# One more step of the first sort on TensorE, 17 fewer scattered columns on GpSimd, and the feed-forward weights loaded earlier, in parts

## The reference

```python
edge_index = jnp.stack([src, dst])
x = x + _L0_gnn_ref(_layernorm(x, axis=-1), edge_index, L0_gnn_W, L0_gnn_a_l, L0_gnn_a_r)   # attention on the graph
x = x + _L0_ffn_ref(_layernorm(x, axis=-1)[None], ...)[0]      # feed-forward on the selected nodes
x = x + _L1_gnn_ref(_layernorm(x, axis=-1), src, dst, edge_type_4, self_W, self_b, rel_W)   # 4 relations
x = x + _L1_ffn_ref(_layernorm(x, axis=-1)[None], ...)[0]      # 8 experts, 2 per node
# attention on the graph, with h = (x @ W) split in 4 heads, row = src and col = dst:
e = jax.nn.leaky_relu(hl[row] + hr[col], negative_slope=ALPHA)
ee = jnp.exp(e - e_max[row])
att = ee / segment_sum(ee, row)[row]
out_h = segment_sum(att[:, :, None] * h[col], row)
# feed-forward: the 1561 of 3125 rows with the greatest weight x @ wr + br
h = gelu(sel @ w1 + b1);  y = (h @ w2 + b2) * w_sel
```

## Time and profile before

| | before |
|---|---|
| median of three runs | 1993.55 us (1991.79 to 1993.94) |
| the profiled execution, own time | 1998.76 us |
| its span | 1997.0 us |
| busy PE / DVE / ACT / POOL | 1437.6 / 1302.2 / 569.5 / 1391.3 us |
| mean granted clock of TensorE | 0.85 of full speed |
| attention's gathers (464) | 447.4 us busy, 964 ns of one |
| scattered columns of sort a (119) | 150.5 us busy, 1265 ns of one |
| chain that ended last | POOL 38%, PE 19%, DVE 17%, issue 15%, DMA 9% |

### The profile page before, as it was taken

The page is one execution under the profiler, slowest core; times in us unless marked ns, Lnnn a source line. Parts: engine busy times, 40 slices in busy tenths (PEclk is TensorE's granted clock), DMA queues, the critical chain, the costliest instruction groups (busy, mean ns, idle before and its releaser), DMA issues.

```text
span 1997.0 us, 22558 instructions
## 1 busy us (share of the span) xinstructions
PE 1437.6 (72%) x6235; PEld 944.4 (47%) x6235; DVE 1302.2 (65%) x2919; ACT 569.5 (29%) x1670; POOL 1391.3 (70%) x1400
## 2 busy tenths in 40 slices
PE   5666267788888887569999967766666776457980
PEld 3333045665565555447775434333333333256870
DVE  6999477788898887475995035445444444666544
ACT  0687211146566663032332311000000000242220
POOL 0788777777777777778875457777777777546771
PEclk9799678889999999779999979889877777557995
DMA  5111034444444444802003573333333333412337
GB/s 92 12 31 28 6 102 108 108 105 118 119 119 118 119 104 119 107 17 62 1 2 83 142 220 105 105 106 105 105 106 106 105 106 104 46 52 72 102 103 213
DMA packets 105960, 183.76 MB, mean 92 GB/s; under 512 B 31722, under 2 KB 70077, under 8 KB 105714
## 3 DMA queue, kind: packets, MB, share of 16 engines
q0 software_dynamic: 56928, 134.61, 27.9%
q1 hardware_dynamic: 47603, 45.16, 8.6%
q10 hardware_dynamic: 1308, 2.56, 0.5%
HBM read 151.56 MB, written 30.39 MB: 91 GB/s over the span
## 4 chain that ended last, share of the span: by engine, by line
POOL 38%; PE 19%; DVE 17%; issue 15%; DMA 9%; DVEq 1%; ACT 1%; SPq 0%; POOLq 0%; ACTq 0%
POOL gath L891 29%; POOL slot_tab L711 8%; PE ps L925 6%; DMA gath<-y_tab,index_b 4%; PE ps L1314 4%; PE ps L1703 2%; DVE hot L1160 2%; DMA gath<-h_tab,index_a 2%; DVE hot L1163 2%; PE ps L1714 2%; DVE gath L964 1%; DVE acc L916 1%; DMA wide<-y_nodes 1%; DVE junk_d L1116 1%; DVE hot_c L637 1%
## 5 line engine op out<-in xcount | busy, mean ns | idle before, releaser
L925 PE MATMUL ps<-gath,hot 128*125 128x260 f32 (+1 forms) x1808 | 615.5, 476 | 297.6 <-DVE gath L964 108.5
L925 PEld LDWEIGHTS ps<-gath,hot 128*125 128x125 f32 x1808 | 354.8, 222 | 518.0 <-DMA gath<-y_tab,index_b 190.5
L891 POOL DMA_INDIRECT gath<-h_tab,index_a x464 | 447.4, 964 | 141.1 <-issue 136.5
L891 POOL DMA_INDIRECT gath<-y_tab,index_b x440 | 416.1, 946 | 166.9 <-issue 121.5
L916 DVE TENSOR_TENSOR acc<-acc,ps 125x257 f32 (+1 forms) x672 | 284.6, 423 | 330.8 <-PE ps L925 303.7
L666 PE MATMUL ps<-hot_c,pay 125*128 125x440 f16 (+1 forms) x884 | 191.9, 370 | 60.3 <-ACT pay L655 60.3
L711 POOL DMA_INDIRECT slot_tab<-sent_word,sent_to x119 | 150.5, 1265 | 87.7 <-DVE sent_to L473 51.8
L721 POOL DMA_INDIRECT slot_tab_b<-sent_word_b,sent_to_b x136 | 164.7, 1211 | 38.8 <-issue 34.5
L655 ACT ACTIVATE pay<-hot_r,plan_b 125x128 f16<-125x128 f16 x578 | 172.0, 386 | 0.0
L666 PEld LDWEIGHTS ps<-hot_c,pay 125*128 125x128 f16 x884 | 86.2, 101 | 157.3 <-ACT pay L655 77.0
L964 DVE TENSOR_TENSOR gath<-gath,ps 128x1024 f32<-128x1024 f32 x116 | 136.0, 1214 | 0.0
(11 more groups left out here) (330 smaller groups left out, 2033.7 us busy)
## 6 DMA issues: line engine op xcount, KB each, us to landing
y_tab<-ybuf SPq DMA_DIRECT2D x25, 448.0 KB
gath<-h_tab,index_a POOLq DMA_INDIRECT x464, 2.8
gath<-y_tab,index_b POOLq DMA_INDIRECT x440, 2.8
h_tab<-hbuf SPq DMA_DIRECT2D x25, 113.8 KB
xa<-in_x SPq DMA_DIRECT2D x1, 2800.0 KB
xa<-in_x SPq DMA_DIRECT2D x5, 560.0 KB
xn_tab<-acc SPq DMA_DIRECT2D x25, 112.0 KB
out<-xa SPq DMA_DIRECT2D x5, 560.0 KB
```

What stands on the lines that cost most here:

```text
L891: p.indirect_dma_start(gath[:, ring(k) + s, 0:width], None, table, bass.IndirectOffsetOnAxis(ap=index[g][:, col:col + 1], axis=0)).then_in ...
L925: ins = t.matmul(ps[0:NP, 4 + q % 2, 0:width], hot[:, s, :], gath[:, s, 0:width], start=(e == 0), stop=(e == n - 1))
```

## The change

`A_STEPS` goes from 18 to 19: TensorE sums 323 columns of sort a, GpSimd sends 102. In `ffn_sync` b1 and br go to the front, as soon as sort b is planned, and the five sets of x, the four parts of w1 and the four of w2 go after the first sums of groups 18, 20, 22, ..., 42, one to every second group, followed by wr and b2. For that, w1_s and w2_s are put where arrays lay that only the planning of the sorts uses, with hid and rel_s behind them.

```diff
-A_STEPS = 18
+A_STEPS = 19
 SENT = EC - A_STEPS * SORT_N
...
     plan = {g: low.tile(f"plan_{g}", [NP, 4, EC]) for g in "ab"}
+    plans_at = low.at
...
+    plans_end = low.at
     unit_tile = low.tile("unit_tile", [1, COLS_B])
...
-    rel_s = mid.tile("rel_s", [128, 2, REL, D])
-    ybuf_at = mid.at
-    hid = mid.tile("hid", [128, HC, U5 * NP])
+
+    w_turned = mid.tile("w_turned", [NT, NP])
+    w_dot, w_col = (mid.tile(n, [NP, NT]) for n in ("w_dot", "w_col"))
+    assert mid.at <= plans_at
+    mid.at = plans_at
     w1_s = mid.tile("w1_s", [128, 2, HID])
     w2_s = mid.tile("w2_s", [128, HC, D])
-    w_turned = mid.tile("w_turned", [NT, NP])
-    w_dot, w_col, gate = (mid.tile(n, [NP, NT]) for n in ("w_dot", "w_col", "gate"))
+    assert mid.at <= plans_end
+    hid = mid.tile("hid", [128, HC, U5 * NP])
+    ybuf_at = mid.at - 4 * U5 * REL * D
+    rel_s = mid.tile("rel_s", [128, 2, REL, D])
+    gate = mid.tile("gate", [NP, NT])
...
-        s.wait_ge(planned, 2)
+        s.wait_ge(words_ready, 2)
+        s.dma_start(b1_s[:, :], b1.rearrange("(k p) -> p k", p=128), allow_slow_non_contiguous=True).then_inc(ffn_in, 16)
+        s.dma_start(br_s[:, :], bcast(br, NP)).then_inc(ffn_in, 16)
+        phase = iter(range(B_PHASE + 2, GROUPS, 2))
+        beside = lambda: s.wait_ge(added["a"], QUADS * next(phase) + 2)
         for i in range(SETS):
-            s.wait_ge(added["a"], QUADS * (B_PHASE + 2 + 5 * i) + 2)
+            beside()
             for lo, hi in SPANS:
                 s.dma_start(xa[lo:hi, set_of(i), :], x_rows[lo:hi, set_of(i), :]).then_inc(x_in, 16)
-
-        s.wait_ge(slots_ready, 2)
-        s.dma_start(b1_s[:, :], b1.rearrange("(k p) -> p k", p=128), allow_slow_non_contiguous=True).then_inc(ffn_in, 16)
-        s.dma_start(br_s[:, :], bcast(br, NP)).then_inc(ffn_in, 16)
         for q in range(4):
-            s.wait_ge(added["a"], QUADS * (B_END + q) + 2)
+            beside()
             s.dma_start(w1_s[:, :, q * D:(q + 1) * D], matrix(w1)[:, :, q * D:(q + 1) * D]).then_inc(ffn_in, 16)
         for q in range(4):
-            s.wait_ge(added["a"], QUADS * (B_END + 4 + q) + 2)
+            beside()
             s.dma_start(w2_s[:, 2 * q:2 * q + 2, :], matrix(w2)[:, 2 * q:2 * q + 2, :]).then_inc(ffn_in, 16)
```

## The result

| | before | after |
|---|---|---|
| median | 1993.55 us (1991.79 to 1993.94, 4 runs) | 1972.44 us (1971.52 to 1974.03, 4 runs) |
| ratio | | 0.9894, 95% interval 0.9881 to 0.9906 |
| profiled execution, span | 1998.76, 1997.0 us | 1972.32, 1970.6 us |
| granted clock of TensorE | 0.85 | 0.861 |

What follows compares the result with a forecast made beforehand. GpSimd's scattered columns of sort a and its gathers of attention were taken as the bound. 14.0 (earlier start) + 2.0 (loads) = 16.0 us less than 1993.55 gave 1977.5 us; own range 1974.5 to 1982, stated range 1969.5 to 1985.5.

Steps and rivals of the forecast that it cites:

- GpSimd's 17 columns: Sort a: with 17 scattered columns less, GpSimd's last ends at 217.08, 25.4 us earlier.
- The step: Sort a: one more step makes VectorE and TensorE the late side; attention's gathers start 14.0 us earlier (12 to 16.3).
- Both bounds: Sort a, beside the 14.0: up to 1.5 us more from TensorE's higher clock, up to 0.8 from scalings beside silent GpSimd.
- The rule on shared ports: Sort a: by the rule added VectorE scalings would hold up GpSimd's columns; the prediction expected 14.0 us or 0.8 more regardless.
- The loads, 2.0 us: Attention's end: moving the loads away saves 2.0 us of gather backlog, 2.6 at most, nothing at least.
- The middle groups, 0: Attention's groups 18 to 42: the loads moved there cost 0, covered by 12.9 us of room.
- rival (3): Attention's middle groups: the moved loads hold the gathers, 5 us slower, 1998.5 us; chance 3%.
- Slow landing by row 0: Attention's end: the last 18 gathers, 128 times row 0 each, land slowly by themselves, 9.3 us instead of 2.8.
- rival (1): Attention's end: the weights alone make landing slow, so it falls from 12.8 to 2.8 us; 24 less, 1969.5; chance 7%.
- "The same 1137 us": From attention's last sum to the kernel's end: the time stays the same 1137 us.
- Rival (2): Sort a's step takes 10.7 us and last gathers stay slow: 12.0 less, 1981.5, or 1985.5 with middle-group loss; chance 5%.
- rival (4): Attention: earlier gathers meet a bound other than GpSimd's issue, so the time stays about 1993; chance 3%.

Runs made afterwards that it cites:

- b_step: The kernel before with A_STEPS = 19 alone, the loads left at their old groups: 1973.86 us, ratio 0.9905.
- c_before: The kernel before, unchanged, run once more with a profile on a slower chip: 2251.19 us.
- b_pads: The changed kernel with the empty slots of the last 64 columns reading 128 different rows: 1968.39 us, ratio 0.9874 to the kernel before.
- b_again: The changed kernel as it is, run once more: 1974.02 us, ratio 0.9897 to the kernel before.
- c_loads: The changed kernel with A_STEPS back at 18, so the moved loads alone, on a slower chip: 2248.14 us, ratio 1.0006 to the kernel before.
- a_again: The changed kernel as it is, run once more on a slower chip: 2233.22 us, ratio 0.992 to the kernel before.
- c_first: The changed kernel with SEND_FIRST = 8 instead of 16, on a slower chip: 2224.36 us, ratio 0.9887 to the kernel before.

## Why the prediction was right, and where it was off

- **GpSimd's 17 columns.** Right: the last ends at 216.97 (217.08 expected), and SyncE reads back at 219.14 (218.7).
- **The step.** The mechanism was right: VectorE and TensorE are the late side. The term was mis-sized, 17.1 us instead of 14.0. VectorE ended at 227.57, not 229.1. The scalings cost 0.32 us each beside a silent GpSimd and 0.37 to 0.39 beside its columns, which makes 1.3 us; I had taken 0.8 us as a bound from the earlier trace rows and left it out. The left scores took 0.35 us less too (1.60 instead of 1.95). Together that is 1.5. TensorE's tail was 1.98 us instead of 3.16, its last batch being at the higher clock (granted 1.00 in 227.6:229.5, where 219.9:223.6 of before has 0.52): 1.2, the other bound I left out. The way from there to the first gather was 2.4 instead of 2.7. Both bounds went one way and neither was in the sum.
- **The rule on shared ports** (the Trainium skill, SBUF — State Buffer, Who interferes with whom). A column is still 1.19 us beside the scalings. But I looked for the price on GpSimd alone; the trace has it on VectorE. By the rule the second of the two to issue is held for the whole instruction of the first; the runs show 0.05 to 0.07 us on a 0.32 us scaling and nothing on a column. That the port is the reason isn't shown.
- **The loads, 2.0 us.** Near in size, and that in part by luck: GpSimd's waits for landings are 2.5 us before and 2.2 in b_step, about 0.8 for each of three parts, and none with the loads moved. The Trainium skill states that DMAs of all issuing engines run on the same 16 DMA engines and interleave (DMA: Bandwidth & Descriptors, Issuing engines are not separate DMA queues); the two traces with such waits agree, the slower chips' show nothing of it (no such waits in c_before). The path was another: I took the last gather's landing and the last sum for the end of the stage, and the columns of sort b for a side that "moves along". b_pads shows the reverse: 9.3 us at the sum changed the additions by 0.3. That the medians moved by it isn't shown: b_step is level with b_again, and on the slower chips the loads give 0.9999 and 1.0006. So the 2.0 us in the sum have no support in the times.
- **The middle groups, 0.** Right: GpSimd stood nowhere between gathers beside a load; 463 starts took 587.85 us against 587.46. That refutes rival (3). wr and b2 are issued 188 and 245 us before their first use, not 400; nothing hung on it.
- **Slow landing by row 0.** An inference then, shown now by b_pads. In after, with no load near, the last gathered rows are still used 10.3 us after the last gather's end (12.8 before); that refutes rival (1), which had 2.8. The forecast didn't hang on it, except that it kept me from expecting 10 us.
- **"The same 1137 us" behind the last sum.** Wrong by 6.5 us: 1130.4 in the pair of profiles. I let everything behind the last sum follow unchanged. That missed TensorE's stand in the feed-forward, which every profile with 18 steps has and none with 19 or 20, and the lower clock behind it: some 3 us (236.8 and 236.9 us from w_tab to hi_b in the two profiles of before, 233.5 in b_step, 233.9 in c_loads). How often the runs of before without a profile paid for that clock isn't on record; their medians lay 5.2 and 4.7 us below the profiled executions. What makes the rest of the 6.5 us stays open.
- **The total.** 1972.44 us lies below the forecast's own range (1974.5 to 1982) and inside the stated one only because that reaches to rival (1), which didn't happen. The steps shown at the additions are 20.0 us, the medians' gain is 21.1. That they meet to 1 us is no proof of the parts: b_again, the same kernel as after, begins its additions 1.6 us later and issues w_tab only 0.3 us later (897.0 against 896.7). Rival (2) fell with the first gather at 231.94, rival (4) with the last, 16.7 us earlier than before.

## What to carry to other kernels

Follow each engine's own row across the border of a stage before you name what ends it: here the last result was not what the next stage waited for, and 9 us won there were worth nothing. A stage behind the change can move too: look for stands of TensorE there, in more than one profile of each kernel. When a bound has a cause that will surely be there (an engine silent, a clock back up), put it into the sum and not beside it. Empty slots of a gather should point to different rows.

## What the hardware did that was not expected

- While gathers of 128 times row 0 were under way (811 to 835 us, b_again), the software queue took 71% of the DMA engines' time and a gather landed in 9.1 us; with 128 different rows (b_pads) 21%, and 2.7 us. At the end of the relations' gathers (1680 to 1685) the DMA share was 0.96 at 83 GB/s, and 0.38 at 105 with the rows spread.
- The same program takes 1994 us in two groups of runs and 2246 to 2251 in two others on other chips, at a mean TensorE clock of 0.85 and 0.81. On the slow ones VectorE, ScalarE and GpSimd stand about 2 us together in nearly every group of attention. VectorE stood 2.00 us for a sum of TensorE beside GpSimd's columns (a_again) and not at all behind them (c_first); that the columns are the reason isn't shown.
- A stand of TensorE of 3.16 us was followed by 6 us at 1.2 GHz in before, and one of 3.18 us by none in c_loads; the 16 matmuls behind it took 6.59 and 3.72 us.
- Behind a row of columns GpSimd started nothing for 6.7 to 6.9 us before its additions (6.89 before, 6.81 after, 6.70 in b_pads, where VectorE's result was 13 us old), and for 5.8 and 5.6 us before the reduction gmax (before, after).
